# Recurrence stage: ten additions per group of tokens on VectorE instead of GpSimd

## The reference

```python
shifted = jnp.pad(h, ((0, 0), (1, 0), (0, 0)))[:, :T_]
delta = shifted - h
x_lerp = h + delta * x_proj_mu
x0 = jnp.tanh(x_lerp @ xl_w1.T) @ xl_w2.T + xl_b2
x1 = jnp.tanh(x0).reshape(B_, T_, 5, R)
x2 = jnp.einsum('btnr,hnr->btnh', x1, x_out_w.reshape(H_, 5, R))
mus = x2 + x_bias
r_mu, w_mu, k_mu, v_mu, g_mu = (mus[:, :, i] for i in range(5))
r = (h + delta * r_mu) @ r_w.T
w_in = h + delta * w_mu
w = jnp.tanh(w_in @ w_w1.T) @ w_w2.T + w_b
k = (h + delta * k_mu) @ k_w.T
v = (h + delta * v_mu) @ v_w.T
g = (h + delta * g_mu) @ g_w.T
...
S = S * w_t[..., None] + k_t[..., None] * v_t[..., None, :]
```

## Time and profile before

| | us |
|---|---|
| median of 3 runs | 5183.19 |
| lowest and highest | 5174.28, 5184.97 |
| the profiled execution, own time | 5169.71 |
| span of its records | 5168.1 |
| TensorE products busy | 4565.2 (88%) |
| VectorE busy | 2719.6 (53%) |
| ScalarE busy | 1988.2 (38%) |
| GpSimd busy | 1665.3 (32%) |

### The profile page before, as it was taken

One profiled execution on the slowest core, in us unless ns is written; L12 is line 12 of the kernel. 1 busy time (PEld: TensorE's weight loads), 2 busy tenths in 40 slices (PEclk: granted clock), 3 DMA queues, 4 the chain that ended last, 5 costly groups with the idle time before them and its releaser, 6 DMA issues. The chain is left out here.

```text
span 5168.1 us, 80399 instructions
## 1 busy us (share of the span) xinstructions
PE 4565.2 (88%) x29148; PEld 3603.7 (70%) x29148; DVE 2719.6 (53%) x5127; ACT 1988.2 (38%) x3685; POOL 1665.3 (32%) x1322
## 2 busy tenths in 40 slices
PE   6605999999999999799999999999997798888885
PEld 6604988988989899466666666666665677777774
DVE  4484333333333343365555555555554477777775
ACT  2203454444444444143333333333333343434431
POOL 1103444434344443332322222322332223333333
PEclk9999999999999999788887888888887899999998
DMA  6622322223232222100000000000000434433432
GB/s 207 219 94 66 50 53 57 44 57 59 39 63 41 60 42 36 32 21 17 22 17 22 17 18 21 22 17 17 21 17 16 132 83 99 97 91 89 99 66 37
DMA packets 246853, 294.07 MB, mean 57 GB/s; under 512 B 19041, under 2 KB 223585, under 8 KB 242401
## 3 DMA queue, kind: packets, MB, share of 16 engines
q0 software_dynamic: 85760, 117.74, 13.3%
q1 hardware_dynamic: 135136, 137.74, 8.3%
q10 hardware_dynamic: 25600, 33.56, 1.9%
HBM read 154.62 MB, written 134.35 MB: 56 GB/s over the span
## 5 line engine op out<-in xcount | busy, mean ns | idle before, releaser
L578 DVE TENSOR_TENSOR e_hTl<-e_hf,e_hTh 128x512 fp32r<-128x512 f32 x512 | 355.0, 694 | 775.0 <-ACT e_hTh L521 774.9
L1031 POOL TENSOR_TENSOR a_mix<-a_tmp,a_h 128x512 f32<-128x512 f32 x320 | 384.1, 1217 | 993.0 <-DVE a_tmp L1090 845.7
L442 POOL DMA_INDIRECT acc_d<-e_y,e_sids x256 | 402.4, 1572 | 723.8 <-DVE e_y L594 678.9
L520 ACT ACTIVATE e_hf<-ps_heads,e_b 128x512 f32<-128x512 f32 x512 | 353.2, 690 | 645.0 <-PE ps_heads L665 641.7
L665 PE MATMUL ps<-e_w2h,e_hTh 128*128 128x256 f32 x2048 | 585.7, 286 | 0.0
L665 PE MATMUL ps<-e_w2h,e_hTl 128*128 128x256 f32 x2048 | 583.6, 285 | 0.0
L665 PE MATMUL ps<-e_w2l,e_hTh 128*128 128x256 f32 x2048 | 577.7, 282 | 0.0
L665 PE MATMUL ps_heads<-e_xTh,e_w1h 128*128 128x512 f32 x1024 | 419.6, 410 | 41.6 <-ACT e_hTh L521 28.9
L665 PE MATMUL ps_heads<-e_xTh,e_w1l 128*128 128x512 f32 x1024 | 408.7, 399 | 0.0
L665 PE MATMUL ps_heads<-e_xTl,e_w1h 128*128 128x512 f32 x1024 | 407.7, 398 | 0.0
L665 PEld LDWEIGHTS ps<-e_w2h,e_hTh 128*128 128x128 f32 x2048 | 392.9, 192 | 19.8
(11 more groups left out here) (287 smaller groups left out, 10089.4 us busy)
## 6 DMA issues: line engine op xcount, KB each, us to landing
r_x<-in_L_attn_hidden_states SPq DMA_DIRECT2D x32, 512.0 KB, 3.8
xn_d<-r_xn ACTq DMA_DIRECT2D x32, 512.0 KB, 3.1
xnT_d<-r_xT ACTq DMA_DIRECT2D x32, 512.0 KB, 3.4
acc_d<-r_zeros POOLq DMA_DIRECT2D x16, 1024.0 KB, 21.1
e_w<-in_L_ffn_w SPq DMA_DIRECT2D x16, 1024.0 KB, 4.9
s_d<-a_s SPq DMA_DIRECT2D x32, 512.0 KB, 2.9
f_a<-acc_d SPq DMA_DIRECT2D x32, 512.0 KB, 3.8
f_x<-s_d SPq DMA_DIRECT2D x32, 512.0 KB, 5.2
```

The lines of the kernel that those rows point to most:

```text
L442: pool.indirect_dma_start(acc_d, bass.IndirectOffsetOnAxis(ap=sids[:, GT * q + t:GT * q + t + 1], axis=0), ys[r][:, t, :], None, compute_o ...
L520: nc.scalar.activation(hf[m % 2][:], ps[2 + m % 2][:], ACT.Gelu, bias=b1s[:, m:m + 1])
L578: nc.vector.tensor_tensor(hT[q % 2][1][:, m, :], hf[m % 2][:], hT[q % 2][0][:, m, :].bitcast(F32), ALU.subtract).then_inc(h_sb, 1)
L1031: nc.gpsimd.tensor_tensor(mix[n][:, m, :].rearrange("p (c t) -> p c t", c=GT), tmp[i % 2][:].rearrange("p (c t) -> p c t", c=GT), h[q % 2] ...
```

## The change

The ten additions of the h row in each group leave GpSimd's `piece` and stand in VectorE's `piece`, behind the loop of products. The two products of a piece come first, then the two additions. GpSimd keeps the subtraction and the reciprocal root. Waits and counts stay what they were, on the other engine.

```diff
             def piece(f, q, s, first):
-                for i in AT.get(s, ()):
-                    n, m = order[i // KD], i % KD
-                    emptied(pool, f, MIX[i])
-                    if not first:
-
-                        last_use = (DLOW, KEY, REC, VAL + 1, GATES + 1)[i // KD]
-                        pool.wait_ge(piece_ps, USES * (f - 1) + last_use + 1)
-                    nc.gpsimd.tensor_tensor(mix[n][:, m, :].rearrange("p (c t) -> p c t", c=GT),
-                                            tmp[i % 2][:].rearrange("p (c t) -> p c t", c=GT),
-                                            h[q % 2][:, m, :, 1:P + 1], ALU.add).then_inc(mixed, 1)
+                pass
...
                     stt(out=tmp[i % 2][:], in0=bank(MIX[i])[:], scalar=xb[:, n, m:m + 1],
                         in1=delta[r][:, m].rearrange("p c t -> p (c t)"), op0=ALU.add, op1=ALU.mult).then_inc(dve_out, 1)
+                for i in AT.get(s, ()):
+                    n, m = order[i // KD], i % KD
+                    emptied(dve, f, MIX[i])
+                    if not first:
+
+                        last_use = (DLOW, KEY, REC, VAL + 1, GATES + 1)[i // KD]
+                        dve.wait_ge(piece_ps, USES * (f - 1) + last_use + 1)
+                    nc.vector.tensor_tensor(mix[n][:, m, :].rearrange("p (c t) -> p c t", c=GT),
+                                            tmp[i % 2][:].rearrange("p (c t) -> p c t", c=GT),
+                                            h[q % 2][:, m, :, 1:P + 1], ALU.add).then_inc(mixed, 1)
```

## The result

The changed kernel takes 5188.2 us (median of 20 executions, 5180.96 to 5194.57) against 5177.27 us (median of 20, 5167.13 to 5184.97) of the kernel before. The ratio is 1.0023, with a 95% interval of 1.0016 to 1.0030: 11 us slower. The profiled execution has a span of 5191.6 us, against 5168.1; with 5193.16 us it was one of the slowest of its 20, while the profiled one of the kernel before, with 5169.71, was one of the faster.

A forecast was written before the change was run, and what follows sets the result against it. TensorE, busy 1794 of 1860 us, was the engine to watch in the recurrence; additions and subtraction were each taken at 0, and zero put on the median of 5183.19 gave 5183 us, with an 8-in-10 range of 5085 to 5245.

The forecast's parts named there:

- the 0.2% that I had set as the bound: Whole kernel: about 0.2% (10 us) is what a measurement can tell from no change; chance of within it 0.46.
- the side to which I had given 0.28: Whole kernel: slower by more than 0.2%, by the moved subtraction, mostly 5200 to 5250 us; chance 0.28.
- the zero: Whole kernel: the summed effect of the change, 0 us, put on the median of 5183.19 us; no change had chance 0.47.
- The additions, slot by slot: VectorE, slots 4 to 8 of the recurrence: 320 additions of 0.68 us, 217 us, lie behind existing waits; cost nothing.
- what GpSimd had held up: VectorE in the recurrence: lines 1137 and 1118 get shorter without GpSimd's additions, 61 us back, leaving about 1168 us busy.
- The subtraction: GpSimd, line 1017: moves from slot 7 to behind the reciprocal root; taken as 0, bounds 0 and 1.8 us a group.
- R would still be reading: VectorE at level 1: R reads until 3019.38 when the subtraction comes, a reason to take its cost as 0.
- the first rival: Recurrence, level 1: subtraction issued ahead of the decay product holds it, 1.77 us a group, 55 us, 5238 us; chance 0.28.
- The groups that draw shifts back: Recurrence: groups repeat at 58.03 us and draw small shifts back, so a few tenths of a microsecond should not show.
- The second rival: Recurrence: TensorE's clock pattern moves, 27 settled groups at 54.26 us, 102 us less, 5081 us; chance of faster 0.25.

The follow-up runs named there:

- first_on_gpsimd_late: Changed kernel with group 0's ten additions back on GpSimd and the subtraction of line 1017 put back behind slot 7's additions: ratio 0.9994 to the kernel before.

## Why the prediction was wrong

No change was forecast, at 5183 us, and there is one: 5188.2 us, a ratio of 1.0023 with an interval clear of 1. It is small, just past the 0.2% that I had set as the bound, on the side to which I had given 0.28. That 5188.2 is so near to 5183 is in part luck: the zero was put on a median of three executions, 5183.19, which over 20 is 5177.27.

**The additions, slot by slot: right.** 0.684 us each, where 0.68 was taken; R and the state's decay at 0.42. VectorE's busy time in the stage is 1123 us where 1168 was forecast. The sum took off too little for what GpSimd had held up: the lerps, which were left out, fell from 1.010 us (in the same view of the kernel before as the earlier trace rows) to 0.746 us, and the 320 additions are 205.5 us, less than 320 x 0.68, since in pairs they overlap. The cost to the path is zero in the full-clock groups with four more products: 50.24 and 50.23 us.

**The subtraction: mechanism right, its place and price wrong.** In the settled groups of the changed kernel it comes 0.27 us behind the decay product (3030.30 against 3030.03), so it was not held, as forecast. That it came out so was luck. My reason, that R would still be reading, had no part in it: counted from the root's start, the decay product now comes at 2.4 to 2.8 us in the settled groups, where it came at 2.96 in the row from which I reckoned. In the second profile's fifth interval, where it comes at 2.94, it is held. In the first profile of the changed kernel none of the 31 intervals has the decay product or the scaling lengthened, in the second one five have. There the first rival is real, with some 3 us in a full-clock group (52.41 against 49.33). In the kernels with four more products it costs 1.42 us in a full-clock group, by the scaling of line 1151 more often than by the decay product that I had named. I had looked only at one settled group. The sum for the rival was off a little too: 3019.27 + 1.89 is 1.86 us behind 3019.30, and not 1.77.

The Trainium skill's rule, in "SBUF — State Buffer", section "Who interferes with whom", that the instruction issued second is blocked for the whole of the first, agrees with this: the scaling, issued 0.33 us behind, ends one undisturbed length (1.25 us, less some 0.2 us of start) behind the subtraction's end.

**The groups that draw shifts back: the step that failed.** I summed over a settled group and multiplied. From the repeating pattern I took that "a few tenths of a microsecond, lost or won, should not show at all", and so the start of the recurrence and the stage behind it got a term of zero without a reason of their own. In the settled groups it held: 58.05 against 58.03 us. Elsewhere it failed. I took the intervals of 49.30 and 54.26 us as a transient that would be there in any case; in one profile of the changed kernel they were gone, which is worth 12.0 us, and in the other they came longer. Moving ten additions in group 0 alone gave 1.0013 (1.0004 to 1.0022). And layer 1, to which the prediction gives no word, took 12 us more in both profiles of the changed kernel. In the first pair of profiles both go with more time at 1.2 GHz: 656 us against 630 in the recurrence, 211 against 182 behind it. Why the clock is low more often there, and how the 11 us of the medians are shared between the two places, no run here shows.

The pattern was also a little less regular than I had read it: 23 of the 31 intervals lie between 58.00 and 58.05 us, the third is 57.68, and the last ones are 58.10, 57.93, 57.74 and 57.83, ahead of the shorter one that ends the stage.

**The second rival,** the clock's pattern, was the right place to look. Its sign was not determined: the same 310 additions gave -0.36% with group 0's ten on GpSimd and +0.2% with them on VectorE.

## What to carry to other kernels

When work is moved off an engine, price what is next in that engine's queue: here the additions were free on VectorE, and it was the subtraction behind them, now early, that cost 1.4 us in a full-clock group. Walk the prologue on its own: here a subtraction that stood behind ten additions was on the path there. Before you read two profiles as two kernels, see where each stands among its kernel's executions. Where the groups of a loop repeat to a few hundredths of a microsecond with the clock falling at one place, a few microseconds of change can turn out with either sign; hold the clock up in both kernels, and then compare them.

## What the runs showed of the hardware that I had not expected

TensorE's clock went to 1.2 GHz for a third of the recurrence (630 of 1852 us) though TensorE was busy over 96% of it by the profile. Four additional products a group, 0.9 us of work, cut this to 120 us and the kernel by 3.2%.

Kernels whose instructions in layer 1 are the same took from 1185.3 us (first_on_gpsimd_late) to 1201.3 us (the changed kernel) from the last reciprocal root to the end, with 168 and 211 us of it at 1.2 GHz.
